# Gated delta-rule scan: each outer product right behind its weights, keys copied for two tokens at a time

## What is computed

```
def step(S, inp):
    q_, k_, v_, b_, a_ = inp
    S = a_[..., None, None] * S
    pred = jnp.einsum('bhkv,bhk->bhv', S, k_)
    S = S + k_[..., :, None] * (b_[..., None] * (v_ - pred))[..., None, :]
    o = jnp.einsum('bhkv,bhk->bhv', S, q_)
    return (S, o)
```

## Time and profile before

| | us |
|---|---|
| median of 3 runs (1989.09 to 1991.72) | 1989.4 |
| span of the profiled execution | 1985.3 |
| outside that span, against the median | 4.1 |
| scan of block 0, and the block change | 119 to 545 |
| scan of block 1, mixed with the post work | 545 to 1082 |
| the second half's post work and the experts | 1082 to 1985 |

### The profile page before, as it was taken

The page is one execution under the profiler, slowest core; times in us unless marked ns, Lnnn a source line. Parts: engine busy times, 40 slices in busy tenths (PEclk is TensorE's granted clock), DMA queues, the critical chain, the costliest instruction groups (busy, mean ns, idle before and its releaser), DMA issues. The chain is left out here.

```text
span 1985.3 us, 28570 instructions
## 1 busy us (share of the span) xinstructions
PE 1381.7 (70%) x6660; PEld 945.6 (48%) x6661; DVE 1274.3 (64%) x3248; ACT 755.7 (38%) x2416; POOL 999.9 (50%) x1214
## 2 busy tenths in 40 slices
PE   6504558700025766667766899998499999999997
PEld 5403446500014554445545667776355555555554
DVE  4599999999989999999987134353322322322322
ACT  5422223501102664565777478886311111111111
POOL 3238888886669997877777425332112112112111
PEclk9757778955557887787887899998699999999999
DMA  4601113520030100010001211143130410411200
GB/s 125 210 5 33 44 38 99 181 106 0 0 132 27 31 26 21 21 36 25 26 26 39 94 32 57 42 137 117 53 110 21 161 58 21 158 61 44 85 16 6
DMA packets 97685, 125.41 MB, mean 63 GB/s; under 512 B 10001, under 2 KB 74952, under 8 KB 95560
## 3 DMA queue, kind: packets, MB, share of 16 engines
q1 hardware_dynamic: 60040, 97.22, 15.3%
q10 hardware_dynamic: 33136, 18.58, 3.2%
q0 software_dynamic: 4432, 8.73, 1.2%
HBM read 89.68 MB, written 35.74 MB: 63 GB/s over the span
## 5 line engine op out<-in xcount | busy, mean ns | idle before, releaser
L208 POOL TENSOR_TENSOR wt<-wt 128x1024 f32<-128x1024 f32 x128 | 304.5, 2379 | 107.8 <-DVE wt L166 107.8
L214 POOL TENSOR_TENSOR wt<-wt 128x512 f32<-128x512 f32 (+2 forms) x384 | 316.9, 825 | 30.1
L1848 PE MATMUL e_ph<-wt,e_g 128*128 x624 | 274.3, 592 | 0.0
L166 DVE SCALAR_TENSOR_TENSOR wt<-wt,scan 128x256 f32<-128x256 f32 x512 | 242.5, 474 | 0.2 <-issue 0.2
L156 DVE TENSOR_TENSOR scan<-scan,wt 128x256 f32<-128x256 f32 x512 | 219.6, 429 | 20.1 <-DVE wt L166 14.0
L147 DVE TENSOR_REDUCE scan<-wt 128x16 f32<-128x272 f32 x512 | 223.2, 436 | 0.1
L135 DVE TENSOR_TENSOR wt<-wt,scan 128x256 f32<-128x256 f32 x512 | 209.9, 410 | 5.4 <-PEq L231 5.4
L1339 ACT ACTIVATE wt<-p_pX,p_mx 128x120 f32<-128x120 f32 x512 | 176.9, 390 | 79.3 <-DVE p_mx L1127 77.9
L1471 PE MATMUL p_pm<-p_w_mix,p_oT 128*128 128x256 f32 x128 | 43.6, 500 | 221.0 <-DMA p_oT<-o 190.7
L1741 POOL TENSOR_TENSOR e_ve<-e_mv,eps 128x1 f32<-128x1 f32 x39 | 7.4, 189 | 368.8 <-DVE e_mv L1792 368.8
L1848 PEld LDWEIGHTS e_ph<-wt,e_g 128*128 128x128 f32 x624 | 115.5, 190 | 130.8 <-issue 130.8
(11 more groups left out here) (220 smaller groups left out, 2920.8 us busy)
## 6 DMA issues: line engine op xcount, KB each, us to landing
wt<-in_L_ffn_W SPq DMA_DIRECT2D x24, 1024.0 KB
qkv<-f_st ACTq DMA_DIRECT2D x48, 256.0 KB, 2.3
p_kE<-kE SPq DMA_DIRECT2D x16, 480.0 KB, 3.7
p_vP<-vP SPq DMA_DIRECT2D x16, 480.0 KB
e_xt<-routed ACTq DMA_DIRECT2D x39, 130.0 KB, 2.1
f_xt<-in_x SPq DMA_DIRECT2D x16, 256.0 KB, 2.8
f_raw_k<-qkv SPq DMA_DIRECT2D x4, 1024.0 KB, 5.3
f_raw_q<-qkv SPq DMA_DIRECT2D x4, 1024.0 KB, 7.8
```

The costliest lines, as they stand in the source:

```text
L166: nc.vector.scalar_tensor_tensor(s["S"][:, h, u], s["S"][:, h, (u - 1) % R], s["gate"][:, jb, h, 1, bass.ds(c * R + u, 1)], s["outer"][:], ...
L208: nc.gpsimd.tensor_tensor(x, s["S"][:, h, z * Q:(z + 1) * Q], s["q"][:, h, now].rearrange("p t (o d) -> p t o d", o=1).to_broadcast([P, Q, ...
L214: nc.gpsimd.tensor_tensor(x[:, :, :, 0:half], x[:, :, :, 0:half], x[:, :, :, half:2 * half], ALU.add).then_inc(s["o_fold"][h], 1)
L1848: ins = nc.tensor.matmul(ph2[:], g1[:, c // (C1 // 2), c % (C1 // 2)], wt[:, bass.ds(at_b + (W2_AT + c * F2), F2)], start=(c == 0), stop=( ...
```

## The change

`scan_step` writes the same instructions in another order, and K copies two tokens' keys instead of four, twice as often, into one half of `kn`. Per token the order is now

```diff
-R, Q, V, KN = 8, 4, 4, 4
+R, Q, V, KN, KB = 8, 4, 4, 4, 2
...
-def next_keys(nc, s, t):
-
-    nc.vector.tensor_copy(s["kn"][:], s["k"][:, :, bass.ds(t, KN)]).then_inc(s["kn_done"], 1)
+def next_keys(nc, s, t, u):
+
+    nc.vector.tensor_copy(s["kn"][:, :, u:u + KB], s["k"][:, :, bass.ds(t, KB)]).then_inc(s["kn_done"], 1)
...
-    if h == 0 and u % KN == 0:
-        dve.wait_ge(s["kn_done"], jb * (TB // KN) + c * (R // KN) + (u // KN + 1))
+    if h == 0 and u % KB == 0:
+        dve.wait_ge(s["kn_done"], jb * (TB // KB) + c * (R // KB) + (u // KB + 1))
...
-    if h == 0 and not (isinstance(c, int) and c == 0 and u == 0):
+    if h == 1 or not (isinstance(c, int) and c == 0 and u == 0):
         dve.wait_ge(s["S_done"], n + 1)
...
     if begun:
-        state_outer(nc, dve, s, jb, *behind, 1)
+        state_update(nc, dve, s, jb, *behind, 1)
     state_weights(nc, dve, s, jb, c, u, 0)
-    if begun:
-        state_update(nc, dve, s, jb, *behind, 1)
-        if u % 2 == 0 and not (last and u == R - 2):
-            next_values(nc, s, vo, t + 2, (u - 2) % V, 2)
+    if begun and u % 2 == 0 and not (last and u == R - 2):
+        next_values(nc, s, vo, t + 2, (u - 2) % V, 2)
     state_outer(nc, dve, s, jb, c, u, 0)
     state_product(nc, dve, s, jb, c, u, 1)
     state_update(nc, dve, s, jb, c, u, 0)
-    if u % KN == KN - 1 and not (last and u == R - 1):
-        dve.wait_ge(s["sk_done"], (c + jb * CHUNKS) * (2 * R) + (2 * u + 2))
-        next_keys(nc, s, t + 1)
     state_weights(nc, dve, s, jb, c, u, 1)
+    if u % KB == KB - 1 and not (last and u == R - 1):
+
+        if not (isinstance(c, int) and c == 0 and u < KB):
+            dve.wait_ge(s["sk_done"], (c + jb * CHUNKS) * (2 * R) + (2 * u - 2))
+        next_keys(nc, s, t + 1, (u + 1) % KN)
+    state_outer(nc, dve, s, jb, c, u, 1)
     if last and u == R - 1:
-        state_outer(nc, dve, s, jb, c, u, 1)
         state_update(nc, dve, s, jb, c, u, 1)
```

More of the change, by code:

```diff
@@ L123, in scan_start @@
 def scan_start(nc, s, vo):
-    next_keys(nc, s, 0)
+    next_keys(nc, s, 0, 0)
     next_values(nc, s, vo, 0, 0, V)
```

## The result

The changed kernel takes 2046.0 us in the median (2043.7 to 2051.0, 4 runs) against 1989.2 us before (4 runs); the ratio is 1.029 with a 95% interval of 1.0272 to 1.0308. That is 57 us slower; 62 were forecast.

What follows compares the result with a forecast made beforehand. VectorE was taken to bound the kernel until 1082 us; 55 us (looped pairs) + 10 (written-out pairs) - 3 (block 1 waits) = +62 on the 1985.3 us span, plus 4.1 outside it: 2051 us, range 2028 to 2066.

Steps and rivals of the forecast that it cites:

- What bounds: Whole kernel: VectorE bounds until 1082 us, each microsecond more there is one more of time; the 903 us behind merely move.
- the wait of the earlier trace: Block 1's scan: VectorE's longest wait for another engine, a TensorE wait of post work, read as 5.3 us.
- The place and its price: Distance W to O, on which everything hangs: 0.68 us in loops with two register instructions bare, 0.48 in written-out code.
- rival 1: Loops: only one of the two register instructions shows, W to O 0.58 us, +40 us, 2030 us; chance 0.12.
- Rivals 1 and 2: The first: see rival 1. The second: no register instruction shows, loops cost as written-out code, +18 us, 2007 us; chance 0.06.
- rival 4: W to O: waiting behind the engine's own last instruction costs nothing, 0.34 us, -18 us, 1971 us; chance 0.05.
- The sum: Whole scan: 55 us for 76 looped pairs, 10 for 52 written-out pairs, 3 off: +62 us, 2051 us.
- a way to be wrong: O to P, P to U, U to W change because the sequencer gets behind with registers after each wait; slower still.
- the term: Written-out code: two tokens take 6.26 us against 6.07, +0.19, for 52 pairs +10 us.
- Block 1: 545 to 1082 us: VectorE busy 504.84 of 537.00 us, so more VectorE time there counts, with 3 us taken off.
- 3 off: Block 1's scan: a later VectorE finds more TensorE-dependent post work ready, so 3 us are taken off.
- Rival 3: Block 1's scan is hidden by post work that waits anyway, only block 0 counts: +40 us, 2030 us; chance 0.07.

## Why the prediction was right, and where its terms were off

**What bounds.** Right: the stretch behind the scan is 899 us against 903, and all of the loss is ahead of it. One reading is off: the wait of the earlier trace rows is not the largest for another engine from 545 to 1082 us, for the first P of block 1 waits 5.4 us for TensorE's sequencer, and the waits for TensorE there are 15.7 us in all.

**The place and its price.** Right: nearly the whole loss of block 0 sits between W and O, 0.68 us in loops and 0.47 in written-out code against 0.68 and 0.48 forecast, and the kernel with one register instruction less behind the wait moved it by 0.08 us, to 0.60, near the 0.58 that rival 1 has for one bare register instruction. Over V, where only one register instruction is there, it is 0.60 in the mean of 39 cases against the 0.58 assumed: 0.56 in two of the three places of a chunk, as from 291.97 to 292.52 us, and 0.68 in the third; why that one is late is open. Rivals 1 and 2 are out by the W to O of 0.67 to 0.70, rival 4 by the same. One pair of numbers shows less than I read in it: the 0.65 and 0.58 us from U1 to O0 are both waits in the sequencer, for in written-out code too the trace has a semaphore instruction there, at 469.10 us in front of the O0 at 469.17. What a late wait in the sequencer costs against one on the instruction is the 0.54 against 0.47 of the swapped waits.

**The sum.** Two looped tokens cost 0.79 us more (3.14 for a chunk) against 0.72 forecast. The missing 0.07 is the loop's branch: 12 times in block 0 the P behind it starts 0.62 to 0.65 us behind O instead of 0.34. My reading is that the sequencer comes to the branch late, because it had to wait itself in front of O1. Before, W1 stood there, with its wait on the reduce itself, and P followed it after 0.34 us, branch or not. I had named such a thing only as a way to be wrong. In written-out code the term was 0.19 and it is 0.10: W to O 0.47, V to O 0.17 and K to O 0.13, each a little less than taken. The two make up for each other in block 0, which is luck: 39.7 forecast (52 x 0.72 + 12 x 0.19), 40.2 measured, of which the loop has 40.9 instead of 37.4, and the three written-out chunks with the block change -0.7 instead of 2.3.

**Block 1.** Forecast 24 x 0.72 + 40 x 0.19 - 3 = 22 us, measured 17.5, though 6.9 us of it are the two idle times of fetching, which I had not forecast at all. Without them the order costs 10 to 11 us there, less than half of the forecast. By place: the 28 written-out pairs ahead of the loop cost 1.6 us, 0.06 each instead of 0.19. Behind the loop 2.9 us are given back (chunks 13 to 15 take 122.3 against 125.2 us), where I had 2.3 for the 12 pairs and 3 off; 1.2 of them are shorter waits for TensorE (7.9 against 9.1 us). The loop's six chunks are 18.8 us longer, of which 12 are left for 24 pairs, 0.5 each instead of 0.72. The kernel with the order alone, which has no such idle times, says the same without a subtraction: its six chunks are 13.5 us longer, 0.56 for a pair, where a pair of its own in block 0's loop costs 0.83 (28.05 against 24.72 us for a chunk). Why is open: the post work between tokens may hide a part of the sequencer's lateness, but no run takes that apart. Rival 3 had a grain of truth: the loop of block 1 hid about a third of its loss. And the 22 us forecast for block 1 look better than they were, since 6.9 us of fetching stand in the 17.5.

The median is 5 us below the forecast. Over both blocks 61.6 us were forecast and 57.7 measured, and that difference is all in block 1. The rest is in the 4.1 us between span and median, which did not stay: with 2044.8 and 2046.0 they are 1.2 us here, since a profiled execution can be faster or slower than the median.

## What to carry to other kernels

Count as a cost what stands between a late semaphore and the instruction that needs it: in a hardware loop, register instructions for addresses and wait numbers wait with it in the sequencer, so the instruction with the tightest dependence should have its wait on itself, in written-out code if need be, and gaps that can't be avoided should be filled with the small copies. The old order had two such gaps in two tokens, each with one bare register instruction; the new one has four, and in 13 of 16 outer products two bare ones. And when a loop's body grows, look in the trace at the first instruction behind its branch and at the instruction queue's packets: a change can pay for fetching that has nothing to do with what it changes.

The best kernel here keeps the old order, copies the keys for two tokens in the gap, and writes out VectorE's loops: 1967.8 us, 0.9916 of the kernel before (0.9898 to 0.9935).

## What the runs showed of the hardware

- VectorE's loop over block 1 is run three times. In some kernels the instruction queue moves 14 packets in that stretch and the branch costs nothing much (334, 335 and 366 traced instructions in a pass), in others 23 to 26, and the first instruction behind the branch comes late, mostly by 2.4 to 3.5 us in each of two passes (342, 343, 346 and 375 instructions). What decides is open: more instructions brought it on in one direct test, but length alone would put 366 on the other side. The Trainium skill, Runtime: NRT & Kernel Launch, section Instruction fetch mechanics, says that an engine's instruction memory holds two blocks and is filled in sequence, and that a taken branch to a target outside them waits for a DMA. The trace agrees in kind: in the changed kernel the sequencer's branch stands at 871.1 us and its next instruction at 874.5, with packets of the instruction queue in between. By that rule it would matter where in the blocks the body begins as much as how long it is; no run here moved the same body to another place.
- A SCALAR_TENSOR_TENSOR of 128 x 256 with two operands in SBUF took 744 ns in the mean over the loop of block 0: 978 where it started beside GpSimd's product with the query, and 475 where no GpSimd instruction ran at its start. With one operand in PSUM it took 474 ns, whatever GpSimd did. In this kernel the wait that a second buffer saves was worth less than that: it ended 48 us slower.
- From reduce to outer product it is 0.47 us with the late wait on the outer product itself, 0.60 with one register instruction bare behind the wait and 0.68 with two, the first of which holds it. A wait on a semaphore instruction of its own, in written-out code, makes it 0.54.
